# A twelve-stage decoder on one core: row means measured ahead, normalisation pairs merged, router logits moved, expert loops written out

## The reference, cut to what matters

```python
def _layernorm(x, axis=-1, eps=1e-05):
    m = jnp.mean(x, axis=axis, keepdims=True)
    v = jnp.var(x, axis=axis, keepdims=True)
    return (x - m) / jnp.sqrt(v + eps)
...
x = _layernorm(x + _L0_attn_ref(x, ...), axis=-1)
x = _layernorm(x + _L0_xattn_ref(x, ctx_768, ...), axis=-1)
x = _layernorm(x + _L0_ffn_ref(x, ...), axis=-1)
...
x = _layernorm(x + _L3_ffn_ref(x, ...), axis=-1)
```

## Time and profile before

| | |
|---|---|
| median of 3 runs | 2713.24 us (2711.34 to 2721.43) |
| the profiled execution | 2733.51 us, span 2731.7 us |
| PE busy | 2131.5 us, 78% of the span; PEld 1291.5 us |
| DVE, ACT, POOL busy | 1618.5, 1175.5, 719.8 us (59%, 43%, 26%) |
| granted TensorE clock, mean | 0.862 |
| DMA | mean 29 GB/s |

### The profile page before, as it was taken

The page is one execution under the profiler, slowest core; times in us unless marked ns, Lnnn a source line. Parts: engine busy times, 40 slices in busy tenths (PEclk is TensorE's granted clock), DMA queues, the critical chain, the costliest instruction groups (busy, mean ns, idle before and its releaser), DMA issues. The chain is left out here.

```text
span 2731.7 us, 38766 instructions
## 1 busy us (share of the span) xinstructions
PE 2131.5 (78%) x12768; PEld 1291.5 (47%) x12768; DVE 1618.5 (59%) x3850; ACT 1175.5 (43%) x2241; POOL 719.8 (26%) x882
## 2 busy tenths in 40 slices
PE   6784696767758886996999998666998896778397
PEld 4562473225632224664545544462343565567254
DVE  4676436998958874445555554454565447366677
ACT  2442336653436663224767766233445322233122
POOL 0430002654311100003655555323443000344000
PEclk7796697997959997998999999785789897789699
DMA  1000000001032200003222221103220001000000
GB/s 36 36 1 6 0 0 5 1 0 51 1 88 63 45 1 1 0 0 96 79 77 79 78 78 29 48 1 79 42 40 2 1 0 65 27 1 1 0 1 15
DMA packets 38149, 80.12 MB, mean 29 GB/s; under 512 B 7296, under 2 KB 21632, under 8 KB 36832
## 3 DMA queue, kind: packets, MB, share of 16 engines
q1 hardware_dynamic: 35520, 75.00, 10.0%
q10 hardware_dynamic: 2464, 3.04, 0.4%
HBM read 51.80 MB, written 7.34 MB: 22 GB/s over the span
## 5 line engine op out<-in xcount | busy, mean ns | idle before, releaser
L680 ACT ACTIVATE spt<-P 128x1024 f32<-128x1024 f32 (+3 forms) x256 | 220.9, 863 | 182.0 <-PE P L537 182.0
L647 DVE TENSOR_REDUCE smf<-P 128x2 f32<-128x1024 f32 (+3 forms) x256 | 255.1, 1019 | 55.0 <-PE P L526 30.6
L2189 PE MATMUL P<-XT,W 128*128 x424 | 219.6, 614 | 61.1 <-ACTq L2223 61.1
L2265 DVE SCALAR_TENSOR_TENSOR X<-P,WE,X 128x128 f32 x576 | 162.2, 344 | 166.6 <-PE P L2206 161.8
L2206 PEld LDWEIGHTS P<-W,e_h 128*128 128x128 f32 (+1 forms) x1952 | 220.4, 190 | 61.0 <-issue 56.8
L2206 PE MATMUL P<-W,e_h 128*128 128x128 f32 (+1 forms) x1952 | 227.5, 277 | 3.4 <-DVE X L2265 3.4
L1027 POOL TENSOR_TENSOR d_e<-d_e,d_rc 128x512 f32<-128x512 f32 (+3 forms) x256 | 179.6, 722 | 176.7 <-DVE d_rc L934 144.1
L2234 ACT ACTIVATE e_g<-P 128x512 f32<-128x512 f32 x148 | 88.4, 597 | 310.5 <-PE P L2189 310.5
L975 ACT ACTIVATE d_e<-d_e,d_mn 128x512 f32<-128x512 f32 (+3 forms) x256 | 141.7, 554 | 132.3 <-DVE d_mn L926 131.9
L2252 DVE TENSOR_TENSOR e_h<-e_g,P 128x512 f32<-128x512 f32 x148 | 101.7, 687 | 108.9 <-PE P L2192 106.8
L554 PE MATMUL P<-spt,sva 128*32 128x256 f32 (+3 forms) x2048 | 151.3, 374 | 4.2 <-ACT soa L686 2.2
(11 more groups left out here) (341 smaller groups left out, 4230.4 us busy)
## 6 DMA issues: line engine op xcount, KB each, us to landing
d_bt<-in_alibi SPq DMA_DIRECT2D x32, 512.0 KB, 3.8
d_moved<-d_raw SPq DMA_DIRECT2D x256, 64.0 KB, 2.0
ska<-parts_k SPq DMA_DIRECT2D x72, 64.0 KB
sqa<-parts_q SPq DMA_DIRECT2D x72, 64.0 KB
W<-in_w_L_xattn SPq DMA_DIRECT2D x1, 4291.0 KB, 14.0
W<-in_w_L_ffn SPq DMA_DIRECT2D x1, 3333.0 KB, 10.7
W<-in_w_L_ffn SPq DMA_DIRECT2D x1, 3155.0 KB, 10.4
parts_k<-sparts SPq DMA_DIRECT2D x8, 384.0 KB, 2.3
```

The lines of the kernel that those rows point to most:

```text
L647: v.tensor_reduce(MF[:, n % 2, u, :], P[:, bank:bank + 2, 0:wide(u)], AX.X, ALU.max, negate=True).then_inc(s("max"), 1)
L680: a.activation(PT[:, n % 3, :, t, N - late(t):N], P[:, BANK_T:BANK_T + 2, 0:late(t)], ACT.Exp, scale=SC).then_inc(s("exp"), 1)
L2189: pe.matmul(P[:, PG + j % 2, :], w["w1"][:, col:col + 128], x, start=True, stop=True).then_inc(s("gate"), 1)
L2265: last = v.scalar_tensor_tensor(x, y, k.WE[:, bass.ds(c * 4 + t, 1), e], x, ALU.mult, ALU.add)
```

## The change

- **Row means ahead.** Each stage measures the rows of `k.X` (or `k.Hs`) right behind the DVE add that finishes them, with the new helper `row_means`; `normalise` no longer measures.
- **Normalisation.** It works in four groups of four tiles, two tiles of each on DVE and two on ACT, with one small chain ahead of them. The last one stores each group by its own transfer.
- **Pairs merged.** Where a stage's own norm followed the norm of the stage before (L0_ffn, L1_ffn, L2_ffn), one `normalise` with `again` computes both scale factors from the same means and variances and writes the twice-normalised tiles. `k.X` itself stays unnormalised; it is brought up to date in the following attention, by ACT in `l0_ffn_attention` and by POOL (`own_rows`) in `self_attention`. 18 runs of `normalise` become 15.
- **Router logits** are computed by PE at the end of the `normalise` ahead of `route`, behind its last transposes.
- **Experts written out**: the two-level loop of `experts` is unrolled into four passes, and its waits are constants.
- **Root table**: each stage's ACT queue ends with a one-element square root (`k.warm`), so that the table is loaded there.

```diff
+def row_means(k, v, s, ST, src, ts, done):
+    if done > len(ts):
+        v.wait_ge(s("row_means"), done - len(ts))
+    for n, t in enumerate(ts):
+        v.bn_stats(ST[:, n, :], src[:, t, :]).then_inc(s("row_stats"), 1)
+    v.wait_ge(s("row_stats"), done)
+    for n, t in enumerate(ts):
+        v.bn_aggr(k.MV[:, t, :], ST[:, n, :]).then_inc(s("row_means"), 1)
...
+            v.reciprocal(inv[:], inv[:]).then_inc(s("inv"), 1)
+            v.wait_ge(s("root"), 1)
+            if not rms:
+                v.scalar_tensor_tensor(nmr[:], mean, -1.0, k.RS[:], ALU.mult, ALU.mult).then_inc(s("nmr"), 1)
+            if again:
+                step(v.tensor_tensor(sq[:], var, k.RS[:], ALU.mult))
+                step(v.tensor_tensor(sq[:], sq[:], k.RS[:], ALU.mult))
+                step(v.tensor_scalar(sq[:], sq[:], again, None, ALU.add))
+                v.reciprocal(sq[:], sq[:]).then_inc(s("inv"), 1)
+                v.wait_ge(s("root"), 2)
+                step(v.tensor_tensor(mul[:], k.RS[:], root[:], ALU.mult))
+                v.tensor_tensor(add[:], nmr[:], root[:], ALU.mult).then_inc(s("nmr"), 1)
+                v.wait_ge(s("nmr"), 2)
+            apply(0)
+            apply(1)
+            apply(2)
+            if not store:
+                copy(1)
+            apply(3)
+            if not store:
+                copy(3)
...
+            stage, width = logits
+            wr, ready = weights(k, stage)
+            ready(pe)
+            for c in QT_:
+                pe.wait_ge(s("xt_a" if c in turned_by_a else "xt_v"), c // 2 + 1)
+                for t in range(4 * c, 4 * c + 4):
+                    pe.matmul(P[:, 7, width * t:width * (t + 1)], k.XT[:, 128 * t:128 * (t + 1)], wr["router"], start=True, stop=True)
+
+def own_rows(k, g, s):
+    for t in range(TILES):
+        g.tensor_scalar(k.X[:, t, :], k.X[:, t, :], k.MV[:, t, 0:1], k.RS[:, t:t + 1], ALU.subtract, ALU.mult).then_inc(s("x"), 1)
...
 self_attention, POOL:
             for n in range(ITEMS + 2):
+                if n == 2:
+                    own_rows(k, g, s)
                 if 0 <= n - 1 < ITEMS:
                     placed(n - 1)
...
 l0_ffn_attention, ACT:
             copies(0)
+            for t in range(TILES):
+                a.activation(k.X[:, t, :], k.X[:, t, :], ACT.Identity, scale=k.RS[:, t:t + 1], bias=k.NM[:, t:t + 1]).then_inc(s("x"), 1)
             for r in range(QT):
...
 context_attention, DVE (the same after every stage's add):
                 v.tensor_tensor(x, x, P[:, 7, 0:128 * c.per], ALU.add).then_inc(s("added"), 1)
+                v.wait_ge(s("added"), n + 1)
+                row_means(k, v, s, ST, k.X, range(c.per * n, c.per * (n + 1)), c.per * (n + 1))
...
 route, PE:
-            for t in range(TILES):
-                last = pe.matmul(P[:, 0, E * t:E * (t + 1)], k.XT[:, 128 * t:128 * (t + 1)], w["router"], start=True, stop=True)
-            last.then_inc(s("logits"), 1)
...
 experts, on PE, ACT and DVE:
-            with pe.Fori(0, 4) as c:
-                x = k.XT[:, bass.ds(c * N, N)]
+            for c in range(4):
+                x = k.XT[:, N * c:N * (c + 1)]
...
 build:
-            normalise(k, i, k.X, k.X, 1e-5, store=i == LAST - 1)
+            if not STAGES[i].endswith("xattn") or STAGES[i] == "L3_xattn":
+                normalise(k, i, k.X, k.X, 1e-5, store=i == LAST - 1, logits=(i + 1, 16) if STAGES[i] == "L3_xattn" else None)
```

230 lines of the change are left out of this document (131 added, 99 removed).

## The result

| | median of the runs | ratio to the kernel before, 95% interval |
|---|---|---|
| before, beside the first series | 2712.89 us (6 runs, 2709.12 to 2721.43) | |
| changed, first series | 2677.57 us (6 runs, 2674.70 to 2694.65) | 0.9873 (0.9856 to 0.9890) |
| changed, second series | 2688.33 us (6 runs, 2674.09 to 2695.70) | 0.9888 (0.9856 to 0.9920) |

The change makes the kernel faster by 1.1 to 1.3%, some 30 to 35 us, about one and a half times the 22.3 that were forecast. The 12 runs of the changed kernel stand in two heaps, seven from 2674 to 2682 and five from 2688 to 2696. The profiled execution took 2677.19 us, its span is 2675.4, the mean granted clock 0.871.

What follows compares the result with a forecast made beforehand. No engine was busy for more than 78% of the span, so a row of phases bounds the kernel. 81.0 us saved less 58.7 paid is 22.3, taken from 2713.2 for 2691 us; range 2668 to 2712.

Steps and rivals of the forecast that it cites:

- the two rivals that ended lower: Row means find cover and POOL is quick, 2670 us, chance 0.12; taken expert branches cost fetches, 2685 us, chance 0.05.
- A plain normalisation, 7.6 us for 10.72.: Seven plain normalisations, without measuring and second chain: 3.1 us saved each, 21.7 in all.
- The pairs: Three merged pairs of normalisations: 9.6 us instead of 22.01, 11.5 saved on each of the other two, 35.4 in all.
- The store: Last normalisation and store: in four pieces, the last transfer carries a quarter and takes 2.8 us, not 4.75; 5.7 saved.
- Norm, logits, routing, 15.4.: Four normalisations ahead of routing, logits moved inside: 4.6 us saved in L0, 4.0 in L1 and L2, 2.8 in L3.
- Experts written out, 2.8.: Start and tail of four expert phases: loop set-up and non-constant waits go, 0.7 us saved four times.
- the rival from the Trainium skill: Expert passes: each of 12 taken branches costs a fetch of 0.5 us, so 6 us more saved, 2685; chance 0.05.
- The last row means, 16.6.: Stage ends: the last group's row means run with nothing beside them, 14.3 us over 11 stages plus four context stages.
- Row means inside the stages, 30.4.: Mid-stage row means on DVE: 17.0 us paid where it has no room, 13.4 where it has some.
- Two fifths for the stages with some room: Cross and self attentions, L2_attn, L3's experts: two fifths of 33.5 us of DVE row means paid, 13.4.
- Bringing k.X up to date, 11.7.: Updates by ACT in l0_ffn_attention, 4.7 us, and by POOL in layer 1 and 2 self attentions, 3 and 4.
- Slower by the clock.: Rival: new DVE instructions in context and self attentions open PE gaps, lowering the clock; over 0.5% slower, 2735 us; chance 0.06.

Runs made afterwards that it cites:

- second profile: The changed kernel, unchanged, run six more times and profiled again; median 2688.33 us, profiled execution 2674.09 us.
- the run with late logits: The changed kernel with the 16 logit products back in the routing, behind a barrier; median 2691.95 us, ratio 0.9893 to the kernel before.
- the run with k.X under cover: The changed kernel with k.X updated in small pieces by ACT and POOL, off the path; median 2672.14 us, ratio 0.9830 to the kernel before.

## Why the prediction was right, and where it was not

The time, 2677.57 for 2691, lies in the range, and faster by over 0.5% was the likeliest case. By the first series the two rivals that ended lower (2670 and 2685) are nearer in size, by the second (2688.33) the forecast is. The sum was too cautious on both sides: the normalisations, routings and the store gave 89.2 us for 78.2, and the stages grew by 51.7 for 55.9. Both go the same way, so the total owes nothing to errors that cancel; among the stages two do in part, the cross attentions with 8.1 less than forecast and layer 2's self attention with 5.3 more.

- **A plain normalisation, 7.6 us for 10.72.** 7.28 by the same measure, first step to last copy, and 7.60 for 11.02 to the next phase. The saving is 3.4 and not 3.1: right, a little small. **The pairs**: 9.36 and 9.2 to the next phase for the 9.6 forecast, 37.2 saved for 35.4. Right. **The store**: 5.7, right.
- **Norm, logits, routing, 15.4.** Logits of 6.84 us inside, as said, but 22.0 saved. The term was too small by what the normalisation itself gains: layers 0 and 1 give 5.2 and 4.7 for the 4.6 and 4.0. Layer 2 gives 7.7, of which 3.1 is the clock: a normalisation with logits takes 13.15 us in layer 1, at a clock of 0.50, and 10.04 in layer 2, at 0.67. In the second profile layer 1's takes 10.05, also at 0.67. L3's 4.4 for 2.8 is the shorter normalisation too. How the gain divides was wrong when I came to test it: in layers 0 and 3, where the clocks are alike, the run with late logits gives 0.3 to 0.6 us to the moving of the logits, not 1.5 to 2, and the rest to the shorter normalisation.
- **Experts written out, 2.8.** 0.2. The step "0.7, four times" took the late start of the loop as lost time; a later part of the phase absorbs it. That the step between passes is worth 0 held, and with it the rival from the Trainium skill (Runtime: NRT & Kernel Launch, Instruction fetch mechanics) fell: the run with loops shows no gap at the pass. The rule speaks of a branch out of the fetched window, and whether these loops leave it no run shows, so the rule itself is not refuted.
- **The last row means, 16.6.** 17.3 by the gaps at the phases' ends. Right.
- **Row means inside the stages, 30.4.** 17 to 25 by the run that measured in the normalisations, 25 by its phases. The step "In L1_xattn a tile costs 0.57 twelve times, at four fifths: 5.5" failed: the whole stage grew by 0.2 to 2.5, as the shift took DVE's two-input instructions away from POOL's. L1's attention (5.4 for 5.5), L3's (4.7 for 4.4) and l0_ffn's were right. Two fifths for the stages with some room was too much for layer 1's self attention and L2's attention (nothing, by the run with k.X under cover in the one and by the second profile, 460.13 for 460.47, in the other) and too little for L0's cross attention (5.0 for 3.2). L2's cross attention got 3.6 shorter (2.3 by the second profile) where 2.2 more were forecast; in the first the clock is 0.82 for 0.78, and the rest stays open.
- **Bringing k.X up to date, 11.7.** 4.2 + 5.9 + 5.9 = 16.0 at the three places, and 13.7 came back by phases when it was put under cover. DVE's idle time grew by 4.2 where 4.7 were forecast. For POOL the size of the tile was off: "so I take 0.6, nearer the first" was wrong, it is 0.793, nearer the upper bound of 0.924, and 16 in a row take 2.8 us more than the 9.6 of the sum; with them the forecast for layer 1 would have been 5.8 for the 5.9 measured. The Trainium skill's rule that one-input work is roughly at line rate on POOL (GPSIMD Engine Reference, Engine selection), from which the prediction took that it would cost nothing, does not hold here: DVE's instruction of the same form takes 0.34 us (six in a row 1.62), POOL's 0.79. What then waits was named rightly, PE for `smb`.
- **Slower by the clock.** Not as a whole, the mean is 0.871. But the clock is the largest thing left out of the sum: it moves one stage by 17.7 us with nothing changed. That the first profile of before was 20 us above its median "and I take the difference over" was the right choice only because 17.7 of them are one stage's clock, which was in no term of the sum; the prediction had nothing that showed this, so it was luck.

## What to carry over

A reduction that every barrier-bound phase begins with belongs behind the instruction that finishes its input; here it cost in the stages some half to three fifths (34 to 42 us) of what it takes in the open (70). Work moved off a critical engine must also leave the queue in front of what others wait for: the same 16 tiles cost PE, which waits for POOL, 5.9 us in one piece, and the wait is gone with two tiles behind each of eight items. Before a few us are read out of two profiles, profile the old kernel twice and compare phases, with the granted clock beside each.

## What the hardware showed that was not expected

- The same program took 265.79 and 248.13 us in one stage, with PE's granted clock at 0.79 and 0.87 and all other engines' busy time equal to 0.5 us.
- DVE's TENSOR_TENSOR of 128 x 616 fp32 values takes 0.80 us alone and 1.27 us when it meets the last 0.62 us of a POOL TENSOR_TENSOR, so DVE can be given 0.5 us of other work for nothing there. Where DVE's starts first, by 0.03 us, it keeps its 0.80 and POOL's of 128 x 308 takes 1.33 for 0.70.
- PE's needless turns in its idle time make the kernel faster: in L3 the normalisation with logits is 8.93 us for 12.10 (clock 1.00 for 0.63), the phase behind L3's attention 7.09 for 10.14 (0.98 for 0.50). In the other three normalisations with logits the same turns left the clock at 0.50 to 0.56 and made the phase 1.5 to 1.7 us longer.
- POOL takes 0.793 us for a tile of 128 x 128 fp32 with one tensor input and two per-row scalars.
